# The second geometry product of a message-passing layer, moved from GpSimd to ScalarE as 24 scaled copies a step

## The reference, cut to what matters

```python
R = relu(abs_distances[:, None] @ w1 + b1) @ w2 + b2
Y = spherical_harmonics(rel_vec)
Fj = features[src]
for i, (mo, lo) in enumerate(RS):
    acc = zeros((E, mo, 2 * lo + 1))
    for j, (mi, li) in enumerate(RS):
        ...
        for k, lf in enumerate(range(abs(lo - li), lo + li + 1)):
            acc = acc + _NORM[i] * einsum('euv,ef,evi,ofi->euo', Rb[..., k], Yf, Fb, C)
out = out.at[dst].add(msg)
```

## Time and profile before

| | before |
|---|---|
| median of 3 runs | 19856.78 us |
| lowest and highest | 19844.69 and 19869.48 us |
| the profiled execution | 19880.46 us |
| its span, first to last instruction | 19878.6 us |
| first and last start of L2498 (416 of them) | 10385.9 and 16053.1 us |
| DVE busy over the span | 16662.2 us (84%) |
| POOL busy | 13030.6 us (66%) |
| PE busy | 9075.4 us (46%) |
| ACT busy | 6250.4 us (31%) |

### The profile page before, as it was taken

One profiled execution on the slowest core, in us unless ns is written; L12 is line 12 of the kernel. 1 busy time (PEld: TensorE's weight loads), 2 busy tenths in 40 slices (PEclk: granted clock), 3 DMA queues, 4 the chain that ended last, 5 costly groups with the idle time before them and its releaser, 6 DMA issues.

```text
span 19878.6 us, 288457 instructions
## 1 busy us (share of the span) xinstructions
PE 9075.4 (46%) x63545; PEld 6845.3 (34%) x63546; DVE 16662.2 (84%) x22374; ACT 6250.4 (31%) x13799; POOL 13030.6 (66%) x13651
## 2 busy tenths in 40 slices
PE   0114110110113777532347777887888864336432
PEld 0114010100113666432235555555555543225322
DVE  9989999999998888755659999999999976665666
ACT  0000233333332555220005555555555553004200
POOL 0048777777777777777757777777777613770476
PEclk9655555555557999555558998888888865555555
DMA  1023444444522222552331111111111165345534
GB/s 18 0 54 24 29 32 33 33 33 30 32 20 50 47 47 47 171 162 69 84 52 13 13 13 13 13 13 13 13 13 13 12 156 188 79 74 190 163 79 68
DMA packets 1751558, 1095.99 MB, mean 55 GB/s; under 512 B 1217323, under 2 KB 1658124, under 8 KB 1750028
## 3 DMA queue, kind: packets, MB, share of 16 engines
q0 software_dynamic: 454272, 412.11, 18.9%
q1 hardware_dynamic: 1089532, 417.46, 8.5%
q10 hardware_dynamic: 207632, 265.14, 4.2%
HBM read 700.94 MB, written 391.12 MB: 55 GB/s over the span
## 4 chain that ended last, share of the span: by engine, by line
POOL 33%; DVE 25%; issue 16%; DMA 13%; DVEq 7%; PE 5%; ACT 1%; POOLq 0%; SPq 0%; ACTq 0%
POOL gat L784 17%; POOL pay L750 12%; DVE red L2516 12%; DMA srcs<-spread,nbx 9%; DVE srcs L2509 5%; DVEq L2515 4%; POOL srcs L806 4%; DMA spread<-srcs 3%; PE banks L1272 3%; DVE arena L1733 2%; DVE srcs L2505 2%; ACT srcs L1016 1%; DVEq L1803 1%; DVEq L2499 1%; DVE g_s L2500 1%
## 5 line engine op out<-in xcount | busy, mean ns | idle before, releaser
L784 POOL DMA_INDIRECT gat<-tab,nbr x3328 | 3511.2, 1055 | 2150.4 <-DMA nbr<-nbr_src 1136.4
L806 POOL DMA_INDIRECT srcs<-spread,nbx x2808 | 2654.7, 945 | 2312.0 <-DMA nbx<-from_src 1375.6
L784 POOL DMA_INDIRECT gat<-tab,pay x3328 | 3172.1, 953 | 1083.7 <-issue 821.4
L1416 PE MATMUL banks<-w2rows,dsts 128*128 128x384 f32 x6656 | 3021.2, 591 | 928.9 <-DVE srcs L2509 739.1
L750 POOL DMA_INDIRECT pay<-records,nbr x2560 | 2523.7, 986 | 798.2 <-issue 779.6
L2516 DVE TENSOR_REDUCE red<-srcs 128x160 f32<-128x2560 f32 x832 | 2346.2, 2820 | 76.1
L1272 PE MATMUL banks<-srcs,hot 128*128 128x96 bf16 (+1 forms) x11232 | 1148.1, 278 | 2742.7 <-DMA srcs<-spread,nbx 2651.4
L1201 PE MATMUL banks<-ident,arena 128*128 128x128 f32 x2240 | 433.2, 380 | 4224.2 <-DVE arena L1761 2807.0
L902 ACT COPY banks<-arena 128x1024 f32<-128x1024 f32 (+1 forms) x1508 | 1323.6, 879 | 3300.8 <-DVE arena L1761 1274.8
L2200 DVE TENSOR_TENSOR arena<-arena,banks 128x96 f32 (+2 forms) x2816 | 723.1, 257 | 1449.0 <-PE banks L1272 1155.5
L1272 PEld LDWEIGHTS banks<-srcs,hot 128*128 128x128 bf16 x11232 | 875.2, 134 | 3015.7 <-issue 1594.9
(11 more groups left out here) (392 smaller groups left out, 20625.4 us busy)
## 6 DMA issues: line engine op xcount, KB each, us to landing
spread<-srcs SPq DMA_DIRECT2D x936, 192.0 KB
dsts<-key_rows SPq DMA_DIRECT2D x234, 512.0 KB
spread<-srcs ACTq DMA_DIRECT2D x468, 204.0 KB
staged<-gat SPq DMA_DIRECT2D x416, 148.0 KB, 1.8
gat<-staged ACTq DMA_DIRECT2D x416, 148.0 KB
dsts<-key_rows ACTq DMA_DIRECT2D x117, 512.0 KB
gat<-tab,nbr POOLq DMA_INDIRECT x3328
gat<-tab,pay POOLq DMA_INDIRECT x3328
```

Of the source, the lines that this page charges most:

```text
L784: pool.indirect_dma_start(out=gatv(s, GC[pas])[:, t, :], out_offset=None, in_=TAB[pas], in_offset=bass.IndirectOffsetOnAxis(ap=row, axis=0 ...
L806: pool.indirect_dma_start(out=chunk_rows(s, c)[:, q, :], out_offset=None, in_=rows, in_offset=bass.IndirectOffsetOnAxis(ap=nbx[:, r, s * X ...
L1416: last = t_.matmul(bank[1 + 2 * (p % 2) + h][:, 0:384], hid_rows[:, s % 2, 2 * p + h, :], w2rows[:, :], start=True, stop=True)
```

## The change

POOL makes only the first product; the count `GEO_OPS` of its signals for each step falls from two to one. ACT makes the second with 24 activations a step: for each of the 8 tiles and each of the 3 components one `Copy` of eight elements, whose scale is a column of `rx` (a per-partition pointer). They stand behind the fourth `keep_sums` and ahead of the eight `Abs` activations. The last of them signals a new semaphore `geo_rest`, for which DVE waits as well before the difference. In the first step of all (`lead`) the wait for `geo_used` is left out.

```diff
-        GEO_OPS = 2
+        GEO_OPS = 1
...
                 g.tensor_tensor(tA, fT[:, b, :, 2:5, :], r_(b, 1), ALU.mult).then_inc(geo_ops, 1)
-                g.tensor_tensor(tB, fT[:, b, :, 1:4, :], r_(b, 2), ALU.mult).then_inc(geo_ops, 1)
...
+            def second_products(n, s, lead):
+                b = s % 2
+                if not lead:
+                    act.wait_ge(geo_used, n)
+                act.wait_ge(geo_ready, 2 * n + 1)
+                for t in range(TPS):
+                    for o in range(3):
+                        last = s_.activation(tB[:, t, o, :], fT[:, b, t, 1 + o, :], ACT.Copy, scale=rx[:, b, t, 2 + o:3 + o])
+                last.then_inc(geo_rest, 1)
+
...
                     keep_sums(n - 2, 3, wins[3])
+                second_products(n, s, lead)
                 for t in range(TPS):
                     last = s_.activation(hot[:, b, t, :], iota[:, :], ACT.Abs, bias=payv(s, PASS_L2)[:, t, 0:1], scale=-1.0)
...
                 dve.wait_ge(geo_ops, (n + 1) * GEO_OPS)
+                dve.wait_ge(geo_rest, n + 1)
                 v.tensor_tensor(g_v[:, b, :, :, 8:16], tA, tB, ALU.subtract).then_inc(geo_used, 1)
```

More of the change, by code:

```diff
@@ L446, in resnorm_gnn_kernel @@
         geo_used = sem("geo_used")
+        geo_rest = sem("geo_rest")
         r_ready = sem("r_ready")
@@ L1069, in step_kept, with radial_round @@
                 act.sem_inc(step_done, 1)
-            def radial_round(i, s, first, final):
+            def second_products(n, s, lead):
[7 more added lines that the diff above has]
+                last.then_inc(geo_rest, 1)
+            def radial_round(i, s, first, final, lead=False):
                 n = i * SLOTS + s
@@ L1117, in _ @@
             for s in range(SLOTS):
-                radial_round(0, s, s < 2, False)
+                radial_round(0, s, s < 2, False, s == 0)
             with act.Fori(1, ITERS - 1) as i:
```

## The result

The changed kernel takes 21279.5 us (median of 4 runs, 21273.3 to 21285.09), the kernel before 19859.51 us beside it; the ratio is 1.0715, 95% interval 1.0698 to 1.0732. It is slower, as forecast, by 1420 us and not by the 558 us of the sum.

A forecast was written before the change was run, and what follows sets the result against it. DVE's own work was taken to bound the step at 13.656 us, with new loops raising it to 15.0: 415 steps add 558 us to 19880.5, giving 20438, less 23.7 for the median: 20415 us, range 20150 to 20760.

The forecast's parts named there:

- What bounds the kernel, and what the removal is worth: DVE's own work sets the 13.656 us step; taking some 0.52 us a step from POOL gains nothing.
- The length of 24 copies: On ACT, the 24 copies take 4.73 us a step, 0.287 us each, starting 0.193 us apart.
- First and second loop: Two dependency loops through the copies exceed DVE's 13.656 us: 15.10 us where PE is slow, 14.78 where it isn't.
- second loop: Copies delay ACT's next round and its window copy, for which PE's sums q = 1 wait: 14.78 us a step.
- first loop: From DVE's difference over PE's p = 2 matmuls, hidden ReLU and copies to the next difference: 15.10 us, 13.47 with fast clock.
- So I expect slow stretches still, but at changing places of the step. I take 15.0 us.: PE's clock stays slow about one stretch a step, at changing places; the step is taken as 15.0 us.
- the clock falls further: Rival, chance 0.08: PE's longer idle time leaves p = 3 and the sums slow too; 15.7 us a step, 20710 us.
- What it adds.: What the change adds on ACT: the time of 24 copies, 4.73 us a step.
- The sum.: 415 steps times (15.0 - 13.656) us add 558 us, giving a median of 20415 us.
- What it delays without cost.: Abs, L1107 and POOL's wait for fT come 4.6 us later, and dT later, all at no cost.
- a DVE that is released by something else: Sign that would show the forecast wrong: DVE's new wait, expected at about 1.3 us a step, not released by ACT's tmpB.

The follow-up runs named there:

- e2_warm: The changed kernel with four filler matmuls a step on TensorE behind the window sums q = 0; 20921.1 us, ratio 1.0526 to the kernel before.
- e8_fewer_warm: The changed kernel with the copies' block made of 13 instructions (second product left out) and four filler matmuls on TensorE; 20320.7 us, ratio 1.0222.
- e9_scratch: The changed kernel, but GpSimd makes both products, the 24 copies go to an unread tile and DVE doesn't wait for them; 21441.6 us, ratio 1.0787.
- e3_fewer: The changed kernel with the copies' block of about the same length made of 13 instructions, second product left out; 20834.4 us, ratio 1.0481.
- e11_split_tmpc: Against the kernel before: 24 copies split over ScalarE's two idle times, GpSimd making DVE's first product instead of the second; 19876.0 us, ratio 1.0000.

## Why the prediction failed, by its own steps

- **What bounds the kernel, and what the removal is worth.** Right. DVE set the step; the product taken from POOL gave nothing back, and POOL's wait for `fT` grew from 0.23 to 4 us a step. DVE's difference takes 358 ns where it took 348, so a product less on GpSimd did not make it faster either.
- **The length of 24 copies.** Right: 4.70 us measured, 4.73 forecast, 0.285 us each; they follow by 0.19. By the figures of the Trainium skill, "ScalarE: Activation LUTs", section "What ACT_TABLE_LOAD costs", an estimated 193 ns lie from start to start. The trace agrees: (4.70 - 0.285) / 23 = 0.192 us.
- **First and second loop.** Right in size: 14.78 us was forecast for the second loop at the fast clock, 14.80 is what three of four steps of e2_warm take, and 14.73 the mean of e8_fewer_warm with a block shorter by 0.13. For the first loop there is the interval of 15.14 us against 15.10; no run tests it alone. e9_scratch showed that the second loop is enough without the first. At the fast clock the block makes 1.07 us of the 3.44.
- **"So I expect slow stretches still, but at changing places of the step. I take 15.0 us."** This step failed. It let the slow clock lengthen p = 2 only. The share became a half, and slow sums, hidden layer and p = 3 lie on the second loop just as p = 2 lies on the first. It costs 1.22 us a step where there is no pause (e3_fewer against e8_fewer_warm). The rival "the clock falls further" was this mechanism, priced at 0.7 us and given 0.08.
- **"What it adds."** It counted the copies' time and not their number as program. This step failed too: 100 more instructions a turn made each loop turn pause for 2.4 us, which none of the rivals had. It adds 1.15 us a step to e3_fewer's 15.95 (or 1.45 with fillers). The pause itself is 2.36 / 4 = 0.6 of it and the longer block up to 0.13; the rest is put down to the slow clock behind the pause, as in the step of e2_warm shown above.
- **The sum.** 13.66 + 1.07 + 1.22 + 1.15 = 17.10 us. The forecast had 1.34 for the first two together and nothing for the third.
- **What it delays without cost.** Wrong in part. `dT` was said to come late at no cost, but PE waits for it in the changed kernel, 58 times and 66.1 us in 234 steps, at the turns. What hangs on the delay of ACT's round is the second loop. The sign of being wrong, "a DVE that is released by something else", came true as well: DVE is also released by PE, 290 us in 234 steps.

What makes the clock stay slow for whole steps, although TensorE is busy in them, was not settled. The runs show only that it goes down behind TensorE's idle time where that was looked at (e2_warm), and that fillers there shorten the slow time: 0.79 without them, 0.99 with them (e3_fewer, e8_fewer_warm).

## What to carry to other kernels

Work that fills an engine's idle time has to stand where that time is: ahead of a wait that the engine has anyway, not behind the result it waited for. ScalarE had 6.3 us idle a step; the same 24 copies cost 3.44 us a step behind the ReLU (with what they set off), 0.85 in one piece in the idle time, and 0.17 split over both gaps. Before many small instructions are put into a loop body, count the body and price them as program too: between 240 and 284 instructions in ScalarE's body lay 2.4 us a turn here. Where a step grows by a wait of TensorE, price its matmuls at the slow clock on every loop, not only where they were slow before.

## What the runs showed of the hardware

- ScalarE's loop body of 284 instructions: 2.36 us (median, the changed kernel) from the end of the branch to the next instruction, medians of 2.36 to 2.50 over all kernels of this kind and single turns of up to 8.3, and 594 or 595 instruction packets (4.87 MB) in the execution. With 184 or 240: 0.18 us, and 87 or 88 packets (0.72 MB or less). All nine kernels with the long body agree, and the five with a shorter one, the kernel before among them.
- A `Copy` of eight columns takes 0.285 us with a pointer as scale, 0.192 with a constant; they follow by 0.19 and 0.10 us. A `Copy` of one column is not cheaper than that: 25 of them fill 2.42 us.
- TensorE was granted 1.2 GHz over 13 us in which it was busy for 12.85 (the changed kernel, from 13000 us); in the kernel before it was granted 1.2 GHz from 12014.6 to 12017.9 us, and 2.4 GHz from 12026 to 12033 us, in which TensorE was busy for 5.20 us of 7.00.
- GpSimd's tensor_tensor over the same 128x192 elements takes 0.54 us for tmpA and 0.72 us for tmpC, whose operand `fT` is read in a permuted order (e11_split_tmpc).
